# Cutting a 256-token tail of a Mamba-2 block into two 128-token halves

## The reference

```
xn     = layernorm(u)                                  # 4096 x 1024
zxbcdt = xn @ in_proj_w.T                              # 4096 x 4240: z 2048, x 2048, B 64, C 64, dt 16
branch(zxbcdt):
    dt     = softplus(dt + dt_bias); A = -exp(A_log)
    x,B,C  = silu(causal_conv4(x,B,C))
    h_t    = h_{t-1} * exp(dt_t*A) + dt_t x_t B_t^T    # 16 heads of 128, state 64
    y_t    = h_t C_t + D x_t
    yz     = y * silu(z)
    return yz * rsqrt(mean(yz*yz) + eps) * norm_w
s   = (branch_fw + reversed branch_bw) @ out_proj_w.T  # 4096 x 1024
g   = silu(fp6_quant(xn) @ fp6_quant(weight).T + bias)
out = u + s * g
```

## Time and profile before

| | |
|---|---|
| median of 3 runs | 7190.3 us (7179.75 to 7198.3) |
| the profiled execution | 7190.82 us, span of its slowest core 7189.3 us |
| spans of the 8 cores | 7152.2 to 7189.3 us |
| mean granted clock of TensorE | 0.591 to 0.594 of full speed |
| busy: PE, DVE, ACT | 2613.6, 2878.6, 1292.9 us |

### The profile page before, as it was taken

The page is one execution under the profiler, slowest core; times in us unless marked ns, Lnnn a source line. Parts: engine busy times, 40 slices in busy tenths (PEclk is TensorE's granted clock), DMA queues, the critical chain, the costliest instruction groups (busy, mean ns, idle before and its releaser), DMA issues.

```text
span 7189.3 us, 45307 instructions; the slowest of 8 cores (7152.2 to 7189.3 us)
## 1 busy us (share of the span) xinstructions
PE 2613.6 (36%) x11656; PEld 1242.1 (17%) x11752; DVE 2878.6 (40%) x5634; ACT 1292.9 (18%) x1843; POOL 125.7 (2%) x234
## 2 busy tenths in 40 slices
PE   0133444443334444014333432522533433352253
PEld 0011122221111222012111211211211211121121
DVE  2533333344333333063344354344345335435432
ACT  0021222221212222011111111111121111111112
POOL 0000000000000000000000000000000000000000
PEclk9955555565555555556556556656656655655655
DMA  4111110110111111710011001001001101110100
GB/s 89 39 34 36 29 28 28 34 34 28 34 36 29 28 28 32 146 42 26 24 35 34 27 25 39 28 18 41 26 21 40 30 22 33 35 32 19 41 26 19
DMA packets 364331, 250.35 MB, mean 35 GB/s; under 512 B 319456, under 2 KB 321761, under 8 KB 355890
## 3 DMA queue, kind: packets, MB, share of 16 engines
q0 software_dynamic: 30448, 132.95, 6.2%
q1 hardware_dynamic: 297216, 74.76, 5.4%
q10 hardware_dynamic: 36418, 39.72, 1.7%
HBM read 117.33 MB, written 68.19 MB: 26 GB/s over the span
## 4 chain that ended last, share of the span: by engine, by line
DVE 31%; PE 29%; DMA 15%; ACT 13%; issue 10%; DVEq 1%; ACTq 1%; POOLq 0%; POOL 0%; SPq 0%
PE ps L239 29%; DVE qv L424 6%; DVE convX L432 3%; DMA u<-u 2%; DMA sflat<-s_scr 2%; ACT convX L797 2%; DVE convX L404 2%; ACT Xtm L1298 2%; ACT convX L509 2%; DMA b3c<-s_scr 2%; DVE convX L410 1%; DVEq L75 1%; DMA stgX<-sp_x 1%; ACT hT L790 1%; DMA ybw<-sp_y 1%
## 5 line engine op out<-in xcount | busy, mean ns | idle before, releaser
L239 PE MATMUL ps<-convBC 64*128 64x128 bf16 x64 | 16.7, 262 | 2572.2 <-DVE um L371 1356.5
L239 PE MATMUL ps<-xnT,warena 128*128 128x256 bf16 (+2 forms) x4480 | 591.1, 294 | 403.1 <-DMA xnT<-xn 197.3
L239 PEld LDWEIGHTS ps<-xnT,warena 128*128 128x128 bf16 (+2 forms) x4480 | 440.1, 105 | 557.1 <-issue 470.0
L424 DVE TENSOR_TENSOR qv<-stgX,cwX 128x1012 bf16<-128x1012 bf16 x384 | 465.5, 1212 | 40.0
L239 PE MATMUL ps<-sflat,ones 3*64 3x512 bf16 (+1 forms) x512 | 282.8, 603 | 484.7 <-ACT mtq L704 245.3
L239 PEld LDWEIGHTS ps<-convBC 64*128 64x128 bf16 x64 | 6.4, 100 | 2588.8 <-issue 2588.8
L239 PE MATMUL ps<-warena,Xtm 128*128 128x512 bf16 x992 | 288.8, 459 | 236.1 <-DVE Xtm L1347 138.1
L709 DVE TENSOR_TENSOR bwq<-Btm,mtq 128x512 bf16<-128x512 bf16 x64 | 44.3, 692 | 796.1 <-ACT mtq L704 796.1
L790 ACT CAST hT<-ps 64x512 bf16<-64x512 f32 x256 | 148.0, 578 | 1015.2 <-PE ps L239 1015.2
L239 PE MATMUL ps<-gcq,hT 64*128 64x128 bf16 x1024 | 290.3, 283 | 0.0
L432 DVE TENSOR_TENSOR convX<-convX,qv 128x1012 bf16<-128x1012 bf16 x384 | 264.7, 689 | 40.1
(11 more groups left out here) (162 smaller groups left out, 4717.7 us busy)
## 6 DMA issues: line engine op xcount, KB each, us to landing
u<-u POOLq DMA_DIRECT2D x64, 512.0 KB, 4.4
sp_x<-stgX POOLq DMA_DIRECT2D x16, 1024.0 KB, 4.2
sp_y<-convX POOLq DMA_DIRECT2D x16, 1024.0 KB, 4.7
stgX<-sp_x POOLq DMA_DIRECT2D x16, 1024.0 KB, 5.7
ybw<-sp_y POOLq DMA_DIRECT2D x16, 1024.0 KB, 5.1
ur<-u POOLq DMA_DIRECT2D x32, 512.0 KB, 4.0
out<-ostg ACTq DMA_DIRECT2D x64, 256.0 KB, 2.1
warena<-ipw POOLq DMA_DIRECT2D x1, 4352.0 KB, 33.2
```

The source lines that it names most:

```text
L239: lambda e: e.matmul(out_ap, lhsT, rhs, start=start, stop=stop),
L424: e.tensor_tensor(scr3, stX[:, t4, isl], sb["cwX"][:, t4, tap:tap + 1].broadcast_to([128, 4, n_main]), op=ALU.mult),
```

## The change

Gating becomes a function of a half s_ of 128 tokens, with all its operations on 128-token slices; the squares go to the same half of Xtm. The program order becomes gating 0, projection 0, gating 1, residual 0, projection 1, residual 1. In the residual both multiplies come first, then add and store for each; the second 512 columns go through u2[:, 0:512] instead of ostg. Projection 1 waits also for the two multiplies of residual 0 (mulv0), since it writes the same PSUM banks. Loads of u2 and ur also wait for all stores so far ("qo"), since u2 is now a source of stores. A block for debugging goes.

```
-                       wait=["tv"], inc="qu", q="gpsimd")
+                       wait=["tv", "qo"], inc="qu", q="gpsimd")     # u2 in both pro(), ur
...
+                def emit_gating(s_):
+                    tsl = slice(s_ * 128, (s_ + 1) * 128)
+                    w1 = [("ts", yfv), "tv"] if s_ == 0 else ["tv"]
+                    ... ystg[:, :, tsl] *= siluz[:, :, tsl]          # DVE, wait=w1
+                    ... ybw[:, :, tsl] *= siluz[:, :, tsl]           # DVE, wait=["tv", "qy"]
+                    gvv = p.mark("tv")
+                    for br, buf in ((0, "ystg"), (1, "ybw")):
+                        p.op("scalar",
+                             lambda e, buf=buf, tsl=tsl: e.activation(
+                                 yzn_ap[:, :, tsl], sb[buf][:, :, tsl],
+                                 AF.Square),
+                             wait=[("tv", gvv), "ts"], inc="ts")
+                        sqv = p.mark("ts")
+                        psl = slice(PB_X + br * G + s_ * 128,
+                                    PB_X + br * G + s_ * 128 + 128)
+                        for i in range(NH):
+                            mm(ps[0:1, psl], sb["ones128b"][:],
+                               yzn_ap[:, i, tsl], i == 0, i == NH - 1,
+                               wait=[("ts", sqv)] if i == 0 else ())
+                        ... Ln, Exp of rrow[0:1, br, tsl]             # ACT
+                    ... two matmuls spread rrow; copy to rbc[:, :, tsl]
+                    ... two multiplies by rbc, add into yzn_ap[:, :, tsl]   # DVE
+                    return p.mark("tv")
+
+                def emit_outproj(s_, ysv_s, extra=()):
...
-                               wait=["tv", "ts"]
+                               wait=[("tv", ysv_s), "ts"] + list(extra)
                                if (k == 0 and nh_ == 0) else ())
+                    opvs[s_] = p.mark("tp")
                     ld(sb["ur"][:], ...
+                       wait=["tv", "qo"], inc="qu", q="gpsimd")
+                    urvs[s_] = p.mark("qu")
+
+                def emit_res(s_):
+                    rdst = [sb["ostg"][:], sb["u2"][:, 0:512]]
+                    for nh_ in range(2):
+                        ... rdst[nh_] = bank * gff
+                             wait=[("tp", opvs[s_]), ("ts", ggv), "tv", "qo"]
+                             if nh_ == 0 else ["tv", "qu"], inc="tv")
+                    mulv = p.mark("tv")
+                    for nh_ in range(2):
+                        ... rdst[nh_] += ur                wait=["tv", ("qu", urvs[s_])]
+                        ... store of rdst[nh_]             wait=[("tv", odv)]
+                    return mulv
+
+                ysv0 = emit_gating(0)
+                emit_outproj(0, ysv0)
+                ysv1 = emit_gating(1)
+                mulv0 = emit_res(0)
+                emit_outproj(1, ysv1, extra=[("tv", mulv0)])
+                emit_res(1)
```

More of the change, by code:

```diff
@@ L1284, in pass_B @@
                 yfv = p.mark("ts")
[L1285 to L1361, removed]
-                        p.op("scalar",
[L1363 to L1366, removed]
@@ L1367, in pass_B @@
-                for s_ in range(2):
+                opvs = [None, None]
+                urvs = [None, None]
+                def emit_gating(s_):
+                    tsl = slice(s_ * 128, (s_ + 1) * 128)
+                    w1 = [("ts", yfv), "tv"] if s_ == 0 else ["tv"]
+                    p.op("vector",
+                         lambda e, tsl=tsl: e.tensor_tensor(
+                             sb["ystg"][:, :, tsl], sb["ystg"][:, :, tsl],
+                             sb["siluz"][:, :, tsl], op=ALU.mult),
+                         wait=w1, inc="tv")
+                    p.op("vector",
+                         lambda e, tsl=tsl: e.tensor_tensor(
+                             sb["ybw"][:, :, tsl], sb["ybw"][:, :, tsl],
+                             sb["siluz"][:, :, tsl], op=ALU.mult),
+                         wait=["tv", "qy"], inc="tv")
+                    gvv = p.mark("tv")
+                    for br, buf in ((0, "ystg"), (1, "ybw")):
+                        p.op("scalar",
+                             lambda e, buf=buf, tsl=tsl: e.activation(
[9 more added lines that the diff above has]
+                               wait=[("ts", sqv)] if i == 0 else ())
+                        rmv = p.mark("tp")
+                        p.op("scalar",
+                             lambda e, br=br, tsl=tsl, psl=psl: e.activation(
+                                 sb["rrow"][0:1, br, tsl], ps[0:1, psl],
+                                 AF.Ln, scale=1.0 / DIN,
+                                 bias=sb["epsb"][0:1, 0:1]),
+                             wait=[("tp", rmv), "ts"], inc="ts")
+                        p.op("scalar",
+                             lambda e, br=br, tsl=tsl: e.activation(
+                                 sb["rrow"][0:1, br, tsl],
+                                 sb["rrow"][0:1, br, tsl],
+                                 AF.Exp, scale=-0.5),
+                             wait=["ts"], inc="ts")
+                    rsv = p.mark("ts")
+                    for br in range(2):
+                        psl = slice(PB_X + br * G + s_ * 128,
+                                    PB_X + br * G + s_ * 128 + 128)
+                        mm(ps[:, psl], sb["ones3"][0:1, :],
+                           sb["rrow"][0:1, br, tsl], True, True,
+                           wait=[("ts", rsv), "tv"] if br == 0 else ())
+                    bcv = p.mark("tp")
+                    p.op("vector",
+                         lambda e, tsl=tsl: e.tensor_copy(
+                             sb["rbc"][:, :, tsl],
+                             ps[:, PB_X:PB_X + 512].rearrange(
+                                 "p (b t) -> p b t", b=2)[:, :, tsl]),
+                         wait=[("tp", bcv)], inc="tv")
+                    rbv = p.mark("tv")
+                    p.op("vector",
+                         lambda e, tsl=tsl: e.tensor_tensor(
+                             sb["ystg"][:, :, tsl], sb["ystg"][:, :, tsl],
+                             sb["rbc"][:, 0:1, tsl].broadcast_to(
+                                 [128, NH, 128]),
+                             op=ALU.mult),
+                         wait=[("tv", rbv)], inc="tv")
+                    p.op("vector",
+                         lambda e, tsl=tsl: e.tensor_tensor(
+                             sb["ybw"][:, :, tsl], sb["ybw"][:, :, tsl],
+                             sb["rbc"][:, 1:2, tsl].broadcast_to(
+                                 [128, NH, 128]),
+                             op=ALU.mult),
+                         wait=["tv"], inc="tv")
+                    p.op("vector",
+                         lambda e, tsl=tsl: e.tensor_tensor(
+                             yzn_ap[:, :, tsl], sb["ystg"][:, :, tsl],
+                             sb["ybw"][:, :, tsl], op=ALU.add),
+                         wait=["tv"], inc="tv")
+                    return p.mark("tv")
@@ L1374, in pass_B @@
                                k == 0, k == 15,
-                               wait=["tv", "ts"]
+                               wait=[("tv", ysv_s), "ts"] + list(extra)
                                if (k == 0 and nh_ == 0) else ())
-                    opv = p.mark("tp")
+                    opvs[s_] = p.mark("tp")
                     ld(sb["ur"][:],
                        dr["u"][t0 + s_ * 128:t0 + (s_ + 1) * 128, :],
-                       wait=["tv"], inc="qu", q="gpsimd")
-                    urv = p.mark("qu")
+                       wait=["tv", "qo"], inc="qu", q="gpsimd")
@@ L1386, in pass_B @@
                              e.tensor_tensor(
-                                 sb["ostg"][:],
-                                 ps[:, pbo:pbo + 512],
+                                 dstb, ps[:, pbo:pbo + 512],
                                  sb["gff"][:, s_, nh_ * 512:(nh_ + 1) * 512],
                                  op=ALU.mult),
-                             wait=[("tp", opv), ("ts", ggv), "tv", "qo"]
-                             if nh_ == 0 else ["tv", "qo"], inc="tv")
+                             wait=[("tp", opvs[s_]), ("ts", ggv), "tv", "qo"]
@@ L1393, in pass_B @@
+                             if nh_ == 0 else ["tv", "qu"], inc="tv")
+                    mulv = p.mark("tv")
+                    for nh_ in range(2):
+                        dstb = rdst[nh_]
                         p.op("vector",
-                             lambda e, nh_=nh_: e.tensor_tensor(
-                                 sb["ostg"][:], sb["ostg"][:],
+                             lambda e, nh_=nh_, dstb=dstb: e.tensor_tensor(
+                                 dstb, dstb,
                                  sb["ur"][:, nh_ * 512:(nh_ + 1) * 512],
@@ L1397, in pass_B @@
                                  op=ALU.add),
-                             wait=["tv", ("qu", urv)], inc="tv")
```

(8 more changed lines are left out.)

4 lines of the change are left out of this document (3 added, 1 removed).

## The result

The changed kernel takes 7051.1 us (median of 8 runs, 7042.4 to 7057.5) against 7187.4 for the kernel before; the ratio is 0.9809, 95% interval 0.9798 to 0.9820.

The account below looks back on a forecast made before the run. No engine bounds the kernel: a nearly serial chain does, with 16 tails of 61.8 us. Each tail gains 4.5 less 0.4 us, 66 in all; less 5 of other costs, 61 us: 7130 us, range 7065 to 7170.

Parts of the forecast that it names:

- the price of the new row sums: Gating's row sums of 16 128-column matmuls: 3.3 us each cold in gating 0, 1.95 warm in gating 1.
- what is hidden: Gating 1's two silu multiplies and first square lie under projection 0; residual 0's adds and stores under projection 1.
- a rival's chance of 0.14: Rival: gating's row sums run at their columns' pace, cold 1.9 and warm 1.1 us; 7058 us, chance 0.14.
- all row sums at their upper bounds: Gating: if every row sum takes its upper bound (3.9 us cold), the kernel takes 27 us more.
- The rest of gating: Half-width pieces: DVE multiply 1.22 us, ACT square 1.91; gating 0 sums to 20.4 us, gating 1's bare part to 12.9.
- The rival of slow slices: Rival: strided half-width slices lose DVE's doubled bf16 rate, 2.3 us instead of 1.22 each; 7267 us, chance 0.05.
- The residual: Tail's residual: store waits leave the path, 1.6 us before projection 1, 3.15 after it; 6.6 us gained a tail.
- Costs beside it: Late ur and stores beside the stgX load, 0.2 us a tail each; POOL waits and last store, 5 us in all.
- Late ur: Second ur load waits for residual 0's stores: 0.2 us a tail; as rival 1.7, about 7155 us, chance 0.12.
- Stores beside the stgX load: At the tail's end both last stores run beside the stgX load: 0.2 us a tail, bounds 0 and 1.2.
- The clock rival: Rival: gating 1's row sums also run at granted clock 0.50, 2.7 us a tail back; 7173 us, chance 0.07.
- The sum: Whole tail of pass B, all pieces added: 57.1 us against 61.6 before, 4.5 us less.

Follow-up runs that it names:

- e9: e7 plus matmuls nobody reads right behind the row sums, 22 in gating 0 and 44 in gating 1: 6848.8 us, ratio 0.9538 to the kernel before.
- e3: Changed kernel, gating 0 row sums with every second matmul on 64 rows (3.17 us a sum) or to another PSUM bank (1.86 us).
- e4: Changed kernel, gating 0 row sums loading 64 columns of ones (1.88 us a sum), or 128 with every second matmul on 64 rows (3.56 us).
- e12: Changed kernel, scan matmuls of equal row count put together and nearly all weight loads 128 columns wide: 6707.1 us, ratio 0.9345 to the kernel before.
- e1: Kernel before with only the new residual (two buffers, multiplies first), gating whole: 7083.4 us, ratio 0.9869.
- e6: Changed kernel, only the ur load no longer waits for the stores: 7024.7 us, ratio 0.9801 to the kernel before.
- e5: Changed kernel plus 48 matmuls nobody reads between gating 1's row sums and projection 1 in each tail: 7031.9 us, ratio 0.9811 to the kernel before.
- after: The changed kernel itself, as profiled, against the kernel before: 7051.1 us, ratio 0.9809.
- e7: Changed kernel, second square in its own buffer, 128-column row sums, shared Ln and Exp, earlier first square and residual 0: 6874.9 us, ratio 0.9590 to the kernel before.
- e10: Changed kernel, scan matmuls reordered so those with equal row count stand together, load widths unchanged: 7048.6 us, ratio 0.9810 to the kernel before.

## Why the prediction was wrong

- **The step that failed: the price of the new row sums.** The mechanism, the order of the chain and what is hidden were right; one term was mis-sized. At a granted clock of 0.50 (cold) I put 0.20 us a matmul, 3.3 us a row sum, and measured 0.107 and 1.88; after a projection, at 1.00 (warm), 0.11 and 1.95, measured 0.056 and 1.07. Two of each per tail: 2 x 1.42 + 2 x 0.88 = 4.6 us, 74 us in 16 tails. 7130 - 74 = 7056, against 7051 measured. That it comes so near is partly luck: so corrected, the forecast has 8.7 us a tail, 139 in all, and the tails gave 7.8, 125 in all; the 11 us ahead of the tails, which nothing in the prediction stands for, fill the gap. The Trainium skill's gap (page "TensorE: Matmul & The Clock Gate", section "Back-to-back issue gap"), which I set against the scan's rows, is what these runs show: about 107 ns cold. Its 81 ns warm for pairs of load and matmul isn't seen here, where 0.056 was measured with loads of one column, and also of 128 (gating 1 in e9: 16 in 1.06 us).
- **Why I chose wrongly.** The earlier trace rows are matmuls of the same width with a load each, but neighbours of different shapes (128*64 and 64*64 stand in those very rows). e3, e4 and e12 show that the change of shape is what costs, not the load. The bound of 0.107 was in the sum as the lower end and had a rival's chance of 0.14; 7065 as the lower limit left it out. (The prediction's 27 us for all row sums at their upper bounds is 24 by its own terms; it changes nothing.)
- **The rest of gating** held: half pieces 1.225 us on DVE (forecast 1.22), 1.909 on ACT (1.91), and gating 0 at 17.7 us, which is the forecast 20.4 less the 2.8 of its row sums. The rival of slow slices is refuted by the 1,225 ns.
- **The residual** held: no store waits, 1.7 us ahead of projection 1 (1.6), 3.3 after it (3.15). e1 gives its worth alone as 6.3 us a tail, of which 1.3 come from a warmer projection 1 that the prediction didn't foresee and that the whole change doesn't get.
- **Costs beside it.** Late ur: forecast 0.2 us a tail; shown 0.9 to 8.2 us in all 16 tails on the eight cores, at most 0.5 a tail, and no more by e6. Stores beside the stgX load: forecast 0.2 us a tail; the load itself goes from 5.7 to 6.4 us (median), but the stretches between tails stay at 191.7 us. The ur load does come last as soon as a projection is faster (e1, e5).
- **The clock rival** is refuted for gating 1's row sums: both run at 1.00 in all tails. But the clock does fall before projection 1, in both kernels, and costs about 2 us there (e5, e9).
- **The sum** of the tail, 57.1 forecast, is 53.7 in the profiled tail; with the true row sums the pieces give 52.5. By the whole chain of that tail the other 1.2 us are 0.5 in gating 1, 0.4 in projection 1, 0.2 in residual 1 and about 0.1 each in gating 0 and residual 0.

## What to carry to other kernels

When a piece that the trace doesn't show is priced by a neighbour's row, compare what stands ahead of each instruction, not only the instruction: here two matmuls of one width differed twofold by the shape of their predecessor. In a serial chain, cutting a stage in two gains what lies under the other half, and what the stages between do to the clock of the next matmuls has to be paid; a gain at one link is real only if the next to arrive, here the ur load, isn't just behind it.

## What the runs showed of the hardware

- Matmuls of 128 columns start 0.107 us apart at a granted clock of 0.50, whatever the width of the weight load (1, 64 or 128 columns: after, e4, e7), and 0.056 at 1.00 (1 or 128 columns: after, e9), as long as neighbours load the same number of rows and of columns. Right behind a slower step it can be 0.08 (e12). Where either changes, the step takes 0.19 to 0.25 us at 0.50 (e3, e4, e10, e12). Another PSUM bank at each step costs nothing (e3: 1.86 us for 16). In this scan equal shapes were worth 344 us of 7051 (e12).
- In the scan, weight loads of 128 columns where 64 were needed made it faster, not slower (e12: a run of 16 in 2.33 or 2.60 us instead of 3.74).
- Ln and Exp on 128 partitions cost what they do on one: 0.48 and 0.42 us for 256 elements in e7, against 0.47 and 0.42 on one partition in the earlier trace rows.
- Matmuls that nobody needs, right behind the row sums, saved 3.9 us a tail (e9): in gating 1 the granted clock stayed at 1.00, in gating 0 it rose from 0.50 to 1.00 while they ran; issued after the clock had fallen, they cost as much as they gave (e5).
